# A perceiver block with a selective scan: the skip term moves from VectorE's first state to TensorE's open sums

## The chip, the core and the metric

The kernel runs on one core of one Trainium2 chip, in one launch. The metric is the device time of an execution in microseconds (us). In the profile PE is TensorE (PEld its weight loads), DVE is VectorE, ACT is ScalarE, POOL is GpSimd and SP is SyncE, which issues most DMAs.

## What is computed

The block has three parts, each with a layernorm before it and a residual after it: cross attention of 64 tokens per batch element on a context of 512 rows (16 batch elements, width 512), a selective scan, and a mixture of 16 experts with 4 chosen per token. The change touches the scan:

```
def step(h, inp):
    x_t, dt, B_t, C_t = inp
    A_disc = jnp.exp(dt[:, :, None] * A[None])
    h = A_disc * h + dt[:, :, None] * B_t[:, None, :] * x_t[:, :, None]
    y_t = jnp.einsum('bds,bs->bd', h, C_t) + D[None, :] * x_t
    return (h, y_t)
...
return y @ out_proj_w.T
```

There are 1024 inner channels and 16 states per channel. So y is a sum of 16 products (state times its C) and of the skip term D * x. All data is fp32.

## The kernel before, in words

**Groups.** The 1024 tokens are worked in four groups of 256. Tokens lie on the free axis and channels on the 128 partitions, so one state of one group is a tile of 128 x 2048 (8 blocks of channels by 256 tokens). The kernel is written out by hand for each engine; each engine has its own program, and semaphores join them.

**The scan of a group runs beside the attention of the next one.** For group g = 0, 1, 2 VectorE does the 16 states of group g while TensorE and ScalarE do the attention of group g + 1. The fourth group's scan runs beside the experts and does its sums on VectorE; it is not touched.

**One state** (scan_step, L1357 on) is on VectorE a product with B (L1365), a scan instruction that takes the decay and the product (L1368), and a product with C (L1372), which overwrites the decay's buffer. ScalarE makes the decay (scan_decay, 8 instructions at L1115). There are three decay buffers, so the decay of state n waits until TensorE has summed state n - 3. SyncE loads the B and C rows of each state (load_bc), two states ahead.

**The sum over states** is on TensorE (sum_state, L674): an identity matmul of the buffer into four PSUM banks, which stay open from the first state to the last. [...] The first state opens the banks (start = True). State 14 is not summed: VectorE adds it to state 15 (join_states, L1391), so a group has 15 sums. ScalarE copies the banks out at the end (copy_sum, L1090) and the output projection (L795) reads that.

**The skip term.** ScalarE writes D * x into th_tmp (y_start, L1082, semaphore ys_rdy). This buffer lies in the same memory as queries_ctx, which the next group's attention will fill. VectorE adds th_tmp to the product of the first state (add_skip, L1386, semaphore skip_added), after it has done states 0 and 1. Two engines wait for skip_added: TensorE before it sums the first state, and ScalarE before it overwrites the memory of th_tmp (L966).

**The order around a boundary**, for the attention of group g + 1:

- TensorE (attn_prep, L627 on): the query projection (16 matmuls, L637), a small key bias product (L643), from the third group on the routing logits of group g - 1 (ffn_logits: transposes L585, matmuls L605), then four steps c = 0 to 3 of the context queries (L665), with the sums of states 0, 1, 2 behind steps 1, 2, 3 (L687). Then two score products (L699) and the sum of state 3, and eight attention units with one sum each (L699, L687, the weighted context L720, the transposes of the probabilities L708).
- ScalarE (attn_prep, L939 on): copies of the queries (L948), the key bias (L981), the routing's copies (L908) and exponential (L923), then per step c the copies of the context queries (L966) and one decay: states 2, 3, 4, 5.
- VectorE: states 0 and 1, add_skip, from the second boundary on the routing of group g - 1 (route, from L1420 on, which waits for ScalarE's L923), states 2 and 3, then one state per unit beside the softmax pieces (L1300, L1304, L1354). In the second unit the slots of the routed tokens are worked out (L1461 to L1472), which wait for TensorE's positions (L621, L622, copied at L933).
- SyncE: the B and C rows wait for the state two before, the context loads for TensorE's scores. GpSimd clears DRAM rows during the first boundary (L1665).

Of the kernel before, what the change touches and what calls it, by code (L numbers as in the profile page):

```python
# [20 lines left out]
ALU = mybir.AluOpType  # L21
# [25 lines left out]
NBK = DI // P  # L47
NS = 16
# [11 lines left out]
GTS = [n * T for n in GBS]  # L60
# [44 lines left out]
JOINED = NS - 2  # L105
PE_SUMS = [j for j in range(NS) if j != JOINED]
NDEC = 3
# [45 lines left out]
def perceiver_block(nc, x, ctx_t, ctx_n, wq_t, wk_w, wv_t, xp_t, dt_t, bc_t, ow_t, gate_t,  # L153
                    eg_t, eu_t, ed_t, params, bc_dram, out):
    with ExitStack() as es:
# [3 lines left out]
        def sem(name):  # L159
            return es.enter_context(nc.semaphore(name))  # L160
# [14 lines left out]
        dA = [dA_[:, s * SW:(s + 1) * SW] for s in range(NDEC)]  # L175
# [8 lines left out]
        ident = par[:, C_ID:C_ID + P]  # L184
# [29 lines left out]
        with ExitStack() as early:  # L214
# [23 lines left out]
            th_tmp = [QT_[:, 3 * SW:3 * SW + NBK * GTS[g]] for g in range(NGR)]  # L238
# [45 lines left out]
        y_bank = bank[2:6]  # L284
# [52 lines left out]
        ys_rdy = sem("y_started")  # L337
# [1 line left out]
        scan_rd = sem("decay_read")  # L339
        step_done = sem("scan_step_done")  # L340
        state_summed = sem("state_summed")
        skip_added = sem("skip_term_added")
        joined = sem("state_joined")
        acc_rdy = sem("y_acc_copied")
        zero_rdy = sem("zero_rows_ready")
# [216 lines left out]
        def _(pe):  # L562
# [67 lines left out]
            def attn_prep(g):  # L630
                if g == 0:
                    pe.wait_ge(wq_in, 16)
                pe.wait_ge(a_free, ja.n)
                for m in range(DC):
                    b = job_a()
                    for c in range(DC):
                        mm = pe.matmul(b[:, 0:GTS[g]], wq[:, c, m * P:(m + 1) * P], xT[g][:, c, :],  # L637
                                       start=(c == 0), stop=(c == DC - 1))
                    mm.then_inc(a_full, 1)
                pe.wait_ge(a_free, ja.n)  # L640
                b = job_a()
                for m in range(DC):
                    mm = pe.matmul(b[0:H, 0:GTS[g]], par[:, C_BK + m * H:C_BK + (m + 1) * H], qT[g][:, m, :],  # L643
                                   start=(m == 0), stop=(m == DC - 1))
                mm.then_inc(a_full, 1)
                if g >= 2:
                    ffn_logits(g - 2)
                if g == 0:
                    pe.wait_ge(wk_in, 16)


                gt = GTS[g]
                pe.wait_ge(d_free, jd.n)
                for c in range(DC):
                    for mp in range(2):
                        if mp == 0:
                            pe.wait_ge(q_free, g * QPAIRS + c)
                            pair = X
                        else:
                            pair = job_a(), job_a()  # L660
                        for k in range(2):
                            m = 2 * mp + k
                            for hh in range(2):
                                r = slice(hh * DH, (hh + 1) * DH)
                                mm = pe.matmul(pair[hh][:, k * gt:(k + 1) * gt], wkt[r, m, c * P:(c + 1) * P],  # L665
                                               qT[g][r, m, :], start=True, stop=True)
                                if mp == 1 and k == 1:
                                    mm.then_inc(a_full, 1)
                        if mp == 0:
                            mm.then_inc(q_full, 1)  # L670
                    if g > 0 and c in (1, 2, 3):
                        sum_state(g - 1, c - 1)
                pe.wait_ge(q_free, (g + 1) * QPAIRS)
                pe.wait_ge(a_free, ja.n)  # L674

            def sum_state(g, j):

                if j == JOINED:
                    return
                if j == 0:  # L680
                    pe.wait_ge(skip_added, g + 1)
                elif j == JOINED + 1:
                    pe.wait_ge(joined, g + 1)
                else:
                    pe.wait_ge(step_done, g * NS + j + 1)
                for c in range(NBK * GTS[g] // 512):
                    mm = pe.matmul(y_bank[c][:, :], ident, dA[(g * NS + j) % NDEC][:, c * 512:(c + 1) * 512],  # L687
                                   start=(j == 0), stop=(j == NS - 1))
                mm.then_inc(state_summed, 1)

            def scores(g, k):
# [191 lines left out]
        def _(act):  # L883
# [60 lines left out]
            def attn_prep(g):  # L944
                for m in range(DC):
                    b = job_a()
                    o = qT[g][:, m, :].rearrange("p (b two i) -> p b i two", two=2, i=TI)
                    act.activation(o, b[:, 0:GTS[g]].rearrange("p (b i two) -> p b i two", two=2, i=TI), ACT.Identity,  # L948
                                   bias=par[:, C_BQ + m:C_BQ + m + 1], scale=DH ** -0.5).then_inc(a_free, 1)
                key_bias(g)  # L950
                if g >= 2:
                    ffn_copy(g - 2)
                    ffn_logits(g - 2)
                if g > 0:
                    act.wait_ge(skip_added, g)
                lead = list(range(2, LEAD + 2)) if g > 0 else []
                if len(lead) > DC:
                    scan_decay(g - 1, lead.pop(0))
                for c in range(DC):
                    q = QT[g][:, :, c, :].rearrange("p u (mp k hh i) -> p mp hh k u i", mp=2, k=2, hh=2)  # L960
                    for mp in range(2):
                        if mp == 0:
                            act.wait_ge(q_full, g * QPAIRS + c + 1)
                        for hh in range(2):
                            b = job_a() if mp else X[hh]
                            ins = act.activation(q[:, mp, hh], b[:, 0:2 * GTS[g]].rearrange("p (k u i) -> p k u i", k=2, u=NUS[g]),  # L966
                                                 ACT.Copy)
                            if mp:
                                ins.then_inc(a_free, 1)
                        if mp == 0:  # L970
                            ins.then_inc(q_free, 1)
                    if lead:
                        scan_decay(g - 1, lead.pop(0))
                assert not lead
# [268 lines left out]
        def _(dve):  # L1243
# [135 lines left out]
                    dve.tensor_tensor(acc_s[g], acc_s[g], h, ALU.add).then_inc(step_done, 1)  # L1379
                    dve.wait_ge(step_done, n + 1)  # L1380

            def add_skip(g):

                h = dA[g * NS % NDEC][:, 0:NBK * GTS[g]]
                dve.wait_ge(ys_rdy, g + 1)
                dve.tensor_tensor(h, h, th_tmp[g], ALU.add).then_inc(skip_added, 1)  # L1386

            def join_states(g):

                a, b = (dA[(g * NS + j) % NDEC][:, 0:NBK * GTS[g]] for j in (JOINED, JOINED + 1))  # L1390
# [181 lines left out]
            for g in range(NGR - 1):  # L1572
                for s in range(LEAD):
                    if s > 0:
                        scan_step(g, s)
                    if s == 1:
                        add_skip(g)
                    if s == 1 and g >= 1:
                        route(g - 1)
                for k in range(NUS[g + 1]):  # L1580
# [163 lines left out]
```

## Time and profile before

| | value |
|---|---|
| median of 3 runs | 1268.64 us (1268.61 to 1268.81) |
| the profiled execution's own time | 1268.13 us |
| its span | 1266.2 us (1.93 us lie around it) |
| instructions | 13226 |
| mean granted clock of TensorE | 0.946 of full speed |
| adds of the skip term (L1386) | 3, 6.9 us in all |
| sums on TensorE (L687) | 45, in 360 rows |

Times in the profile are microseconds from the span's start. A row of the timeline gives start, length, engine, line, operation and tiles, and in brackets how long the engine was idle before it and what it waited for. The chain of waits is followed back from the last instruction: at each step it names the piece of work that released the next one. The granted clock of 1.00 is 2.4 GHz for TensorE and 0.50 is 1.2 GHz; a value between is a mean over a stretch with both. A matmul's recorded end is modelled, so starts are the safer numbers on that engine.

### The profile page before, as it was taken

How to read it: one execution, taken by the hardware profiler on the slowest of the kernel's cores; microseconds unless marked ns; L12 is line 12 of the kernel's file. 1: busy time of each engine (PE TensorE's matmuls, PEld its weight loads, DVE VectorE, ACT ScalarE, POOL GpSimd, SP SyncE). 2: the span in 40 equal slices, each digit the busy share in tenths (PEclk: the TensorE clock that was granted, in tenths of full speed). 3: DMA queues.
4: the chain of work that ended last, by engine and by line, in shares of the span. 5: the costliest groups of instructions: out<-in, count | busy, mean ns of one | idle time of the engine just before them, and what ended most of it. 6: DMA issues, size and time to landing. Idle time of an engine off the chain costs nothing.

```text
span 1266.2 us, 13226 instructions
## 1 busy us (share of the span) xinstructions
PE 1109.1 (88%) x4228; PEld 711.6 (56%) x4228; DVE 895.3 (71%) x960; ACT 625.2 (49%) x1378; POOL 134.4 (11%) x113
## 2 busy tenths in 40 slices
PE   6997879998999999999799895459999999899992
PEld 4885646775755676656577582325544445454451
DVE  1312589999889999989989996569999956133312
ACT  4552676563666565586466454424555313222230
POOL 0001111000100340000070000210000002043002
PEclk9998889999999999999999998569999999999997
DMA  8368566768601454500344320279999957999994
GB/s 296 117 208 310 200 227 211 257 225 286 221 11 24 131 163 115 151 8 19 75 154 129 110 67 9 74 273 338 371 362 349 370 228 263 381 379 408 411 351 130
DMA packets 115187, 266.25 MB, mean 210 GB/s; under 512 B 11280, under 2 KB 44208, under 8 KB 115120
## 3 DMA queue, kind: packets, MB, share of 16 engines
q1 hardware_dynamic: 99248, 207.22, 47.9%
q0 software_dynamic: 15872, 58.20, 12.0%
q8 instruction: 34, 0.56, 0.2%
q14 instruction: 33, 0.27, 0.1%
HBM read 197.07 MB, written 68.32 MB: 210 GB/s over the span
## 4 chain that ended last, share of the span: by engine, by line
PE 55%; DVE 30%; ACT 6%; DMA 5%; issue 3%; POOL 1%; SPq 1%; POOLq 0%; DVEq 0%; ACTq 0%
PE bank L816 11%; DVE state L1368 10%; PE bank L777 9%; PE bank L720 6%; PE bank L699 6%; PE bank L837 6%; PE bank L687 6%; DVE state L1365 5%; PE bank L795 3%; DVE decay L1372 3%; PE bank L748 3%; DVE state L1375 2%; ACT decay L1115 2%; DMA queries_ctx<-in_xp_t 2%; DVE y_acc L1379 2%
## 5 line engine op out<-in xcount | busy, mean ns | idle before, releaser
L1368 DVE TENSOR_TENSOR_SCAN state<-decay,state 128x2048 f32<-128x2048 f32 x64 | 282.9, 4421 | 9.5 <-ACT decay L1115 8.6
L816 PE MATMUL bank<-expert_w,block_x_t 128*128 128x512 f32 x496 | 227.0, 601 | 3.8 <-ACT block_x_t L1171 3.8
L687 PE MATMUL bank<-decay,params 128*128 128x512 f32 x360 | 163.5, 600 | 4.5 <-DVE decay L1372 4.5
L816 PEld LDWEIGHTS bank<-expert_w,block_x_t 128*128 128x128 f32 x496 | 91.4, 194 | 95.7 <-issue 91.2
L1674 POOL DMA_INDIRECT dispatched<-ffn_x,slot x32 | 74.1, 2316 | 662.6 <-DVE slot L1472 654.0
L1115 ACT ACTIVATE decay<-delta_even,params 128x256 f32<-128x256 f32 x256 | 107.2, 498 | 49.4 <-PE bank L687 47.2
L720 PE MATMUL bank<-probs,ctx 128*128 128x256 f32 x512 | 121.3, 392 | 7.7 <-ACT probs L1012 7.7
L1527 DVE SCALAR_TENSOR_TENSOR hidden<-hidden,bank 128x256 f32<-128x256 f32 x62 | 26.1, 421 | 138.2 <-ACT hidden L1175 137.1
L699 PE MATMUL bank<-ctx,queries_ctx 128*128 128x256 f32 x512 | 118.3, 386 | 2.2 <-issue 1.2
L1115 ACT ACTIVATE decay<-delta_odd,params 128x256 f32<-128x256 f32 x256 | 106.2, 499 | 28.4 <-PE bank L687 25.1
L837 PE MATMUL bank<-expert_w,hidden_t 128*128 128x512 f32 x248 | 117.0, 594 | 2.9 <-ACT hidden_t L1185 2.9
L720 PEld LDWEIGHTS bank<-probs,ctx 128*128 128x128 f32 x512 | 100.4, 197 | 32.3 <-issue 10.0
L777 PE MATMUL bank<-normed_t,queries_ctx 128*128 128x256 f32 x512 | 112.1, 381 | 1.1 <-DMA queries_ctx<-in_xp_t 1.1
L687 PEld LDWEIGHTS bank<-decay,params 128*128 128x128 f32 x360 | 67.8, 192 | 77.5 <-issue 70.9
L1372 DVE TENSOR_TENSOR decay<-state,bc_bcast 128x2048 f32<-128x2048 f32 x48 | 109.5, 2281 | 0.7
L699 PEld LDWEIGHTS bank<-ctx,queries_ctx 128*128 128x128 f32 x512 | 97.3, 194 | 17.1 <-issue 3.1
L777 PEld LDWEIGHTS bank<-normed_t,queries_ctx 128*128 128x128 f32 x512 | 97.3, 191 | 16.4 <-DMA queries_ctx<-in_xp_t 2.5
L1175 ACT ACTIVATE hidden<-bank 128x256 f32<-128x256 f32 x62 | 23.7, 382 | 148.1 <-PE bank L816 148.1
L837 PEld LDWEIGHTS bank<-expert_w,hidden_t 128*128 128x128 f32 x248 | 46.8, 190 | 61.1 <-issue 57.4
L1181 ACT ACTIVATE block_y<-bank 128x512 f32<-128x512 f32 x62 | 37.1, 598 | 82.0 <-PE bank L837 82.0
L1365 DVE TENSOR_TENSOR state<-u_even,bc_bcast 128x2048 f32<-128x2048 f32 x32 | 73.3, 2291 | 4.0 <-DMA bc_bcast<-bc_scratch 3.1
L1365 DVE TENSOR_TENSOR state<-u_odd,bc_bcast 128x2048 f32<-128x2048 f32 x32 | 73.3, 2290 | 2.4 <-DMA bc_bcast<-bc_scratch 1.6
(192 smaller groups left out, 1327.9 us busy)
## 6 DMA issues: line engine op xcount, KB each, us to landing
dispatched<-ffn_x POOLq DMA_DIRECT2D x38, 1024.0 KB, 5.3
expert_w<-in_eg_t SPq DMA_DIRECT2D x62, 512.0 KB, 6.3
expert_w<-in_eu_t SPq DMA_DIRECT2D x62, 512.0 KB, 10.0
expert_w<-in_ed_t SPq DMA_DIRECT2D x62, 512.0 KB, 10.0
ctx<-in_ctx_t SPq DMA_DIRECT2D x32, 512.0 KB, 7.2
ctx<-in_ctx_n SPq DMA_DIRECT2D x32, 512.0 KB, 3.8
bc_bcast<-bc_scratch SPq DMA_DIRECT2D x64, 256.0 KB, 6.4
block_x<-dispatched SPq DMA_DIRECT2D x62, 256.0 KB, 9.8
```

What stands on the lines that cost most here:

```text
L687: mm = pe.matmul(y_bank[c][:, :], ident, dA[(g * NS + j) % NDEC][:, c * 512:(c + 1) * 512], start=(j == 0), stop=(j == NS - 1))
L699: mm = pe.matmul(o, QT[g][:, k, c, qb * P:(qb + 1) * P], ctxT[n % 2][:, c, :], start=(c == 0), stop=(c == DC - 1))
L720: mm = pe.matmul(b[:, cc * Q:(cc + 1) * Q], ctxN[n % 2][:, j, c * P:(c + 1) * P], probT[n % 2][:, j, :], start=(j == 0), stop=(j == KC - 1))
L748: mm = pe.matmul(b[hh * DH:(hh + 1) * DH, 0:GTS[g]], wv[:, c, h * DH:(h + 1) * DH], QT[g][:, :, c, h * TI:(h + 1) * TI], start=(c == 0), s ...
L777: mm = pe.matmul(b[:, kk * gt:(kk + 1) * gt], w[:, c, (k + kk) * P:(k + kk + 1) * P], xT[g][:, c, :], start=(c == 0), stop=(c == DC - 1))
L816: mm = pe.matmul(o, xbT[q % 2][:, c, :], w_gu[q % NW][:, :, c, :], start=(c == 0), stop=(c == DC - 1))
L837: mm = pe.matmul(bank[4 + q % 2][:, :], hidT[q % 2][:, c, :], w_dn[q % NW][:, c, :], start=(c == 0), stop=(c == IC - 1))
L1115: ins = act.activation(dA[n % NDEC][:, k * gt:(k + 1) * gt], dlt[g][:, k, :], ACT.Exp, scale=par[:, c:c + 1])
L1365: step(dve.tensor_tensor(h3, u[g], bs, ALU.mult))
L1368: dve.tensor_tensor_scan(h, dA[n % NDEC][:, 0:sw], h, 0.0, ALU.mult, ALU.add).then_inc(scan_rd, 1)
L1372: dve.tensor_tensor(hc, h3, cs, ALU.mult).then_inc(step_done, 1)
L1674: pool.indirect_dma_start(xd[WAVE_OF[c]], bass.IndirectOffsetOnAxis(slot[:, i:i + 1].bitcast(U32), 0), fx[:, t, :], None).then_inc(dispatc ...
```

## The change

The add of the skip term on VectorE is taken out, with its semaphore. TensorE puts th_tmp itself into the four banks with the identity, as an opening sum (start_sum), and the first state's sum is then added as the others are. The opening sum stands behind the key bias product and ahead of the routing logits. ScalarE no longer waits for skip_added before it fills queries_ctx; it waits for TensorE's context queries as before, and these stand behind the opening sum in TensorE's order. The joining of states 14 and 15 stays.

```
--- before.py
+++ after.py
@@ -339,7 +339,6 @@
-        skip_added = sem("skip_term_added")
@@ -643,6 +642,8 @@  (attn_prep of TensorE)
                 mm.then_inc(a_full, 1)
+                if g > 0:
+                    start_sum(g - 1)
                 if g >= 2:
                     ffn_logits(g - 2)
@@ -673,19 +674,23 @@
+            def start_sum(g):
+
+                pe.wait_ge(ys_rdy, g + 1)
+                for c in range(NBK * GTS[g] // 512):
+                    pe.matmul(y_bank[c][:, :], ident, th_tmp[g][:, c * 512:(c + 1) * 512], start=True, stop=False)
+
             def sum_state(g, j):
 
                 if j == JOINED:
                     return
-                if j == 0:
-                    pe.wait_ge(skip_added, g + 1)
-                elif j == JOINED + 1:
+                if j == JOINED + 1:
                     pe.wait_ge(joined, g + 1)
                 else:
                     pe.wait_ge(step_done, g * NS + j + 1)
                 for c in range(NBK * GTS[g] // 512):
                     mm = pe.matmul(y_bank[c][:, :], ident, dA[(g * NS + j) % NDEC][:, c * 512:(c + 1) * 512],
-                                   start=(j == 0), stop=(j == NS - 1))
+                                   start=False, stop=(j == NS - 1))
@@ -951,8 +956,6 @@  (attn_prep of ScalarE)
-                if g > 0:
-                    act.wait_ge(skip_added, g)
@@ -1378,12 +1381,6 @@
-            def add_skip(g):
-
-                h = dA[g * NS % NDEC][:, 0:NBK * GTS[g]]
-                dve.wait_ge(ys_rdy, g + 1)
-                dve.tensor_tensor(h, h, th_tmp[g], ALU.add).then_inc(skip_added, 1)
@@ -1573,8 +1570,6 @@  (main loop of VectorE)
                 for s in range(LEAD):
                     if s > 0:
                         scan_step(g, s)
-                    if s == 1:
-                        add_skip(g)
                     if s == 1 and g >= 1:
                         route(g - 1)
```

## Rows read from the trace of the kernel before

**Rows 1.** The page: busy time by engine, and the chain by engine.
```profile
PE 1109.1 (88%) x4228; PEld 711.6 (56%) x4228; DVE 895.3 (71%) x960; ACT 625.2 (49%) x1378; POOL 134.4 (11%) x113
...
PE 55%; DVE 30%; ACT 6%; DMA 5%; issue 3%; POOL 1%; SPq 1%; POOLq 0%; DVEq 0%; ACTq 0%
```

**Rows 2.** The instruction groups by line, of lines L687 and L1386.
```profile
L687 PE MATMUL bank<-decay,params 128*128 128x512 f32 x360 | 163.5, 600 | 4.5 <-DVE decay L1372 4.5
...
L1386 DVE TENSOR_TENSOR decay<-decay,queries_ctx 128x2048 f32<-128x2048 f32 x3 | 6.9, 2292 | 0.1
```

**Rows 3.** Chain of waits, stretch 150 to 300: shares, then start, length, piece.
```profile
by line: PE bank L687 23.3%; PE bank L699 18.3%; PE bank L720 17.4%; DVE state L1368 5.9%; DMA ctx<-in_ctx_t 5.9%; PE bank L748 5.2%; ACT decay L1115 4.4%; PE bank L665 4.0%; DVE decay L1372 3.1%; PE bank L708 1.9%; DVE u_even L1344 1.6%; D
...
176.52 2.30 DVE decay L1386
...
178.84 1.09 ACT queries_ctx L966 x2
...
179.98 2.21 PE bank L665 x16
...
203.88 3.45 PE bank L687 x8
```

**Rows 4.** Timeline, first boundary: start, length, engine, line, [idle before <- releaser].
```profile
160.43 3.28 ACT L1082 ACTIVATE queries_ctx<-queries_ctx,params 128x256 f32<-128x256 f32 x8
...
175.26 1.89 PE L643 MATMUL bank<-q_t,params 128*8 128x256 f32 x8 [0.82 <-ACT q_t L948]
...
177.09 2.01 PE L665 MATMUL bank<-q_t,attn_weights 64*128 64x256 f32 x16
...
180.77 3.30 ACT L1115 ACTIVATE decay<-delta_even,params 128x256 f32<-128x256 f32 x8
...
184.17 4.42 DVE L1368 TENSOR_TENSOR_SCAN state<-decay,state 128x2048 f32<-128x2048 f32 x1 [3.16 <-ACT decay L1115]
```

**Rows 5.** Timeline, second boundary, at the routing.
```profile
372.93 1.89 PE L643 MATMUL bank<-q_t,params 128*8 128x256 f32 x8 [0.80 <-ACT q_t L948]
...
378.14 2.29 DVE L1386 TENSOR_TENSOR decay<-decay,queries_ctx 128x2048 f32<-128x2048 f32 x1
...
379.13 0.20 ACT L923 ACTIVATE route_logits<-bank 128x32 f32<-128x32 f32 x1 [0.91 <-PE bank L605]
...
380.35 0.17 DVE L1420 TENSOR_SCALAR route_score<-route_logits 128x32 f32<-128x32 f32 x1
```

**Rows 6.** Timeline, third boundary, at the routing.
```profile
585.12 2.29 DVE L1386 TENSOR_TENSOR decay<-decay,queries_ctx 128x2048 f32<-128x2048 f32 x1
...
585.96 0.20 ACT L923 ACTIVATE route_logits<-bank 128x32 f32<-128x32 f32 x1 [0.71 <-PE bank L605]
...
587.33 0.17 DVE L1420 TENSOR_SCALAR route_score<-route_logits 128x32 f32<-128x32 f32 x1
```

**Rows 7.** Timeline, second group: the third state's sum, a transpose, the slots.
```profile
398.05 5.40 PE L687 MATMUL bank<-decay,params 128*128 128x512 f32 x8 [2.03 <-DVE decay L1372]
...
416.38 1.12 PE L708 MATMUL bank<-params,probs 128*128 128x128 f32 x4 [2.59 <-ACT probs L998]
...
429.84 0.19 DVE L1464 TENSOR_TENSOR route_position<-route_position,iota_f 128x32 f32<-128x32 f32 x1 [1.87 <-ACTq L935]
```

**Rows 8.** Timeline, third group: the same transpose.
```profile
623.07 0.66 PE L708 MATMUL bank<-params,probs 128*128 128x128 f32 x4 [3.99 <-ACT probs L998]
```

**Rows 9.** Chain of waits, whole run: the score matmuls behind those transposes.
```profile
210.57 3.46 PE bank L699 x16
...
417.50 4.57 PE bank L699 x16
...
623.72 5.14 PE bank L699 x16
```

**Rows 10.** Windows: PE, PEld, DVE, ACT, POOL busy, clock, DMA share, GB/s.
```profile
440.00:480.00 40.00, 39.87 (x163) 29.11 (x162) 39.31 (x29) 24.27 (x63) 18.48 (x6) 1.00 0.61 178
...
585.00:590.00 5.00, 5.00 (x31) 3.87 (x32) 4.66 (x18) 2.83 (x7) 0.00 (x0) 0.69 0.27 56
```

## The prediction, made before the changed kernel ran

> **What bounds the kernel now.** I read the page first, then the chain of waits, then the timeline of the three places where the change acts. The page gives PE 88% busy and DVE 71%, and the chain of the whole run is 55% PE and 30% DVE [rows 1]. So neither engine bounds alone, and an add taken from DVE and given to PE must be priced place by place. The add is made three times, 2.29 us each, and a sum on PE is eight rows of the trace [rows 2]; in an unbroken stream such a sum takes 3.45 us of PE's time [rows 3]. The change therefore trades 6.9 us of DVE for about 10.4 us of PE. Who is waited for at each of the three boundaries decides.
>
> At the **first boundary** the chain goes from the add (176.52) by ScalarE's copy (178.84) to PE at 179.98, and from there the stretch to 300 is mostly PE: its L687, L699 and L720 hold 59% of it [rows 3]. PE is what must not be delayed here. At the **second and third** the chain is DVE's: state 1, the add, the routing, states 2 and 3, without a gap that I can find up to the slots in the second unit. Here one looks at what DVE does next after the add: the routing's first instruction, L1420, which needs ScalarE's exponential L923, which needs PE's logits. The add ends at 380.43 and L1420 starts at 380.35 (the engine's pipeline overlaps them); L923 has ended at 379.33, only a microsecond before [rows 5]. At the third boundary it is 587.41, 587.33 and 586.16 [rows 6]. So the logits are nearly late already, and the change puts the opening sum ahead of them on PE.
>
> **First boundary, step by step.** The skip term is ready at 163.7 [rows 4], so the opening sum does not wait for it. The key bias product starts at 175.26 and the context queries follow it at 177.09 [rows 4]. The opening sum goes between them: 177.1 to 180.55. Step c = 0 then starts at 180.55 and has its first half (half of 2.01 us) done at 181.6. Today that half is done at 178.1, and ScalarE's copies begin at 178.84, held for 0.7 us by the add. So they would begin at about 181.7, and PE's step 1, which today starts at 179.98, 1.14 us behind them, would start at 182.85: **+2.9 us**. What is late next: the decay of state 2, today at 180.77, stands behind those copies on ScalarE and moves by 2.9 us too; DVE, which already waits 3.16 us for it at 184.17 [rows 4], then waits 2.9 + 2.3 us longer. Its own saving of 2.3 us is lost in that wait, and states 2 and on are 2.9 us late together with PE. The sums of states 0, 1 and 2 move by the same amount, none waits for another reason. Everything down to the group's end follows PE; I count 2.9 us in full. SyncE's loads of B and C and of the context wait for DVE's steps and PE's scores, so they move along; the key bias rows come from ahead of the opening sum and do not. GpSimd's clearing paces itself and costs nothing new.
>
> **Second boundary.** PE is at the key bias product at 372.93, with 1.89 us of it, and goes on to the routing's transposes [rows 5]. The skip term has long been there. With the opening sum ahead of them, transposes, ScalarE's copies, logits and L923 all come 3.45 us later: 379.33 becomes 382.8, and L1420 starts about 0.1 us behind, at 382.9 instead of 380.35: **+2.5 us** on DVE, which has been idle since 378.1. The 2.29 us saved turn into a wait of 4.8 us. Behind it the routing, state 2 and state 3 are 2.5 us late. PE's context queries are 3.45 us late, but PE waits 2.03 us for state 2 at 398.05 anyway [rows 7], so DVE's 2.5 us rule from there. At 416.38 PE waits 2.59 us for probabilities that hang on DVE's row sums and on the decay behind PE's fourth sum [rows 7], of which the second is a few tenths later; PE loses some 2.3 us there. In the units both engines are full: PE 39.87 of 40 us, DVE 39.31 [rows 10]. Nothing can catch up. I take **+2.4**.
>
> **Third boundary.** L923 ends at 586.16 and would end at 589.6; L1420 goes from 587.33 [rows 6] to 589.7: **+2.4**. The wait at 623.07, 3.99 us [rows 8], is for DVE alone, so it passes the delay on whole. ScalarE's wait for the add goes too, but it was held there for at most a tenth.
>
> **The sum** is 2.9 + 2.4 + 2.4 = 7.7 us. The taken-out add is worth nothing at all three places, since its engine waits for ScalarE or for the routing there. The first state's sum only changes its start flag, and joining, copying out and the output projection are as before: nothing. In the last group and the experts no instruction changes; they start later by the sum. Against the profiled execution, 1268.13 us, that is 1275.8 us; the median of the runs is 0.5 us above the profiled one, so **1276.3 us**.
>
> **Bounds of the unshown cost.** No row shows an opening sum at this place. From above: a sum at a lowered clock is also there, 5.40 us at 398.05 [rows 7], 1.95 us more than 3.45. At the routing each such case would cost 1.95 us. From below: zero, if PE did it in its own gaps. It can't, as PE works in order, but it is an end. I take 3.45 for all three: PE had been busy with dense matmuls just before. With zero at all three the change would gain: 0.7 us at the first boundary (the hold of the copies), 380.35 - 379.4 = 0.9 and 587.33 - 586.2 = 1.1 us, 2.7 us together.
>
> **A rule on the clock.** PE's granted clock is 0.69 between 585 and 590, just behind the broken run of small products and waits [rows 10], and the score matmuls behind the waits of 2.59 and 3.99 us take 4.57 and 5.14 us where an undisturbed set takes 3.46 [rows 9]. The opening sum adds 3.45 us of dense matmuls to that broken run and could keep the clock up; what that would give is rival B. The Trainium skill (TensorE: Matmul & The Clock Gate, the table "Why this matters for your kernels") says that idle gaps between bursts of matmuls let the clock fall back to half. By that rule this change would win some of these microseconds back; the trace agrees that they are lost today.
>
> **The rivals.**
>
> *A, forecast: PE's new sum is paid at all three places.* +7.7, 1276.3. Against it: it needs full occupation up to the slots. Its own range is 1274 to 1278.5.
>
> *B: the clock gives back.* If the sum keeps PE at full clock, L699 behind the two waits takes 3.46 instead of 4.57 and 5.14 [rows 9]: 1.1 and 1.7 us less. DVE waits 1.87 us for PE at the slots at 429.84 [rows 7], so it would pass on. +7.7 - 2.8 = +4.9, 1273.5. Against it: those waits are for DVE, and they get longer by the change, not shorter.
>
> *C: the sum itself runs at half clock* at the two routing places, +2 x 1.95 = +3.9: +11.6, 1280.2. For it: clocks do fall near there. Against: they fall after it.
>
> *D: hidden at the routing.* If DVE's delay were taken up by its wait of 1.87 us at the slots and its twin, only 0.5 us would be left at each of the two, and 2.9 at the first: +3.9 or less, down to no change if the first is also half hidden; 1269 to 1272. Against it: that wait is for positions that PE makes after the delayed probabilities.
>
> *E, the other side: faster.* The mechanism is the release of DVE. It is decided at L1420: if the logits are there at 378.1, DVE goes on at once. They come at 379.33 even without the opening sum, so the most is the 2.7 us above: 1265.9. It needs PE to have room for 3.45 us ahead of the logits, and its gap ahead of the key bias product is 0.80 us long [rows 5].
>
> *F: it does not do what it says*, a sum that is left out or done twice. The banks are opened once and the sixteen terms are still added; twelve new matmuls, 24 rows. I give it no chance of its own.
>
> **How the numbers follow.** A 0.70, B 0.11, C 0.07, D 0.09, E 0.03. What a measurement of this kernel can tell from no change is 0.2%, 2.5 us, so 1266.1 to 1271.2. All of A, B and C lie above: 0.88, with 0.02 of D 0.90 for slower. The rest of D is within: 0.07. E reaches the lower bound just so: 0.03 for faster. The range takes in A, B and most of C, and reaches down to the upper part of D: 1272 to 1280.
>
> **What would show it.** In the changed profile: L687 in 360 rows as before and a new line of 24, about 3.45 us for each eight; no L1386; at the first boundary PE's step 1 at about 182.9 and DVE's scan of state 2 at about 187.1 behind a wait of some 8 us; at the two others an idle DVE of 4.6 to 4.9 us ahead of L1420, and L1420 2.4 to 2.5 us later relative to the boundary. From the routing of the second boundary to that of the third it is 206.98 us today [rows 5, 6] and would be about 209.4. It is wrong if L1420 is not idle before it (then the logits don't wait for PE's order), if PE's units no longer fill, or if the experts' part changes in length by over a microsecond, since nothing there is touched.

## The result and the profile after

The changed kernel takes 1274.74 us, the kernel before 1269.05 us (medians of 20 runs each, taken side by side). The ratio is 1.0048, with a 95% interval of 1.0031 to 1.0064: 6.1 us slower, between 3.9 and 8.1 (the medians themselves are 5.7 us apart). Forecast were 7.7 us and 1276.3. Both kernels scatter more over 20 runs (1261 to 1272 and 1270 to 1279) than the first three runs of the kernel before showed. The profiled execution of the changed kernel took 1271.51 us, its span is 1269.6.

The page of the changed kernel, busy time and chain by engine. Its line numbers differ from those of the kernel before by three fewer to five more (the sum of a state, L687, is L692, the routing's first instruction, L1420, is L1417):

```profile
PE 1115.6 (88%) x4252; PEld 713.8 (56%) x4252; DVE 888.7 (70%) x957; ACT 624.2 (49%) x1378; POOL 134.2 (11%) x113
...
PE 62%; DVE 22%; ACT 6%; DMA 5%; issue 3%; POOL 1%; SPq 1%; POOLq 0%; DVEq 0%; ACTq 0%
```

The groups of instructions by line, TensorE's old and new sums:

```profile
L692 PE MATMUL bank<-decay,params 128*128 128x512 f32 x360 | 163.5, 600 | 3.6 <-DVE decay L1375 3.6
...
L681 PE MATMUL bank<-queries_ctx,params 128*128 128x512 f32 x24 | 11.1, 605 | 0.0
```

VectorE has three instructions and 6.6 us less, TensorE 24 rows more [rows 1, 2], two for each of the twelve matmuls. They take 11.1 us, of which TensorE's busy time shows 6.5, since other matmuls ran faster in this execution; and the chain has gone over to TensorE. The trade is the one forecast; the three places show what it costs.

The timeline of the first boundary (start, length, engine, line, idle time before):

```profile
174.19 1.89 PE L642 MATMUL bank<-q_t,params 128*8 128x256 f32 x8 [0.80 <-ACT q_t L953]
176.02 3.70 PE L681 MATMUL bank<-queries_ctx,params 128*128 128x512 f32 x8
179.65 2.00 PE L666 MATMUL bank<-q_t,attn_weights 64*128 64x256 f32 x16
180.83 2.06 ACT L969 ACTIVATE queries_ctx<-bank 128x512 f32<-128x512 f32 x4 [4.07 <-PE bank L666]
186.15 4.42 DVE L1371 TENSOR_TENSOR_SCAN state<-decay,state 128x2048 f32<-128x2048 f32 x1 [6.75 <-ACT decay L1118]
```

ScalarE's copies (L969) no longer wait for VectorE but for TensorE's context queries, which stand behind the sum (L681), and VectorE waits 6.75 us for the decay of state 2 instead of 3.16 [rows 4]. The waits are those that the forecast named, but TensorE's step 1 starts at 181.97 instead of 182.85, and VectorE's wait is 6.75 us instead of some 8.

The second boundary and the third (the sum's row is 3.70 us long with its modelled end, but the next row starts 3.54 us behind its start):

```profile
375.23 3.70 PE L681 MATMUL bank<-queries_ctx,params 128*128 128x512 f32 x8
...
378.77 1.04 PE L584 MATMUL bank<-params,ffn_x 128*128 128x128 f32 x8
...
382.65 0.20 ACT L928 ACTIVATE route_logits<-bank 128x32 f32<-128x32 f32 x1 [0.77 <-PE bank L604]
383.00 0.18 DVE L1417 TENSOR_SCALAR route_score<-route_logits 128x32 f32<-128x32 f32 x1 [4.42 <-ACTq L930]
...
400.71 3.70 PE L692 MATMUL bank<-decay,params 128*128 128x512 f32 x8 [1.05 <-DVE decay L1375]
...
592.69 0.18 DVE L1417 TENSOR_SCALAR route_score<-route_logits 128x32 f32<-128x32 f32 x1 [4.41 <-ACTq L930]
...
610.41 5.40 PE L692 MATMUL bank<-decay,params 128*128 128x512 f32 x8 [2.54 <-DVE decay L1375]
```

VectorE had no idle time ahead of the routing [rows 5, 6]; now it waits 4.42 and 4.41 us there for the logits. Against the start of the output projection before it (L795, now L800), the routing begins 31.53 and 31.55 us on, where it was 29.36 and 29.39: **2.2 us late at both**.

### The profile page after: what moved, and what is told of

Same layout as the page of the kernel before. It is cut to its first block, busy times and chain, and to the rows that moved or that the text cites. A ratio compares the mean times of both kernels' runs of the same rounds, so it can differ in the third digit from the quotient of the medians.

```text
span 1269.6 us, 13268 instructions
## 1 busy us (share of the span) xinstructions
PE 1115.6 (88%) x4252; PEld 713.8 (56%) x4252; DVE 888.7 (70%) x957; ACT 624.2 (49%) x1378; POOL 134.2 (11%) x113
## 4 chain that ended last, share of the span: by engine, by line
PE 62%; DVE 22%; ACT 6%; DMA 5%; issue 3%; POOL 1%; SPq 1%; POOLq 0%; DVEq 0%; ACTq 0%
PE bank L821 11%; PE bank L782 9%; DVE state L1371 7%; PE bank L692 7%; PE bank L725 7%; PE bank L704 7%; PE bank L842 6%; DVE state L1368 4%; PE bank L800 3%; PE bank L753 3%; PE bank L636 2%; ACT decay L1118 2%; DVE state L1378 2%; DMA queries_ctx<-in_xp_t 2%; DVE y_acc L1382 2%
## 5 line engine op out<-in xcount | busy, mean ns | idle before, releaser
L1371 DVE TENSOR_TENSOR_SCAN state<-decay,state 128x2048 f32<-128x2048 f32 x64 | 282.9, 4420 | 13.1 <-ACT decay L1118 12.2
L692 PE MATMUL bank<-decay,params 128*128 128x512 f32 x360 | 163.5, 600 | 3.6 <-DVE decay L1375 3.6
L725 PE MATMUL bank<-probs,ctx 128*128 128x256 f32 x512 | 117.9, 384 | 8.0 <-ACT probs L1015 8.0
L704 PE MATMUL bank<-ctx,queries_ctx 128*128 128x256 f32 x512 | 120.0, 390 | 1.3 <-issue 1.2
L725 PEld LDWEIGHTS bank<-probs,ctx 128*128 128x128 f32 x512 | 98.0, 192 | 31.7 <-issue 10.0
L692 PEld LDWEIGHTS bank<-decay,params 128*128 128x128 f32 x360 | 67.8, 192 | 76.5 <-issue 70.9
L704 PEld LDWEIGHTS bank<-ctx,queries_ctx 128*128 128x128 f32 x512 | 98.8, 197 | 16.6 <-issue 3.1
```

The source lines that it names most:

```text
L704: mm = pe.matmul(o, QT[g][:, k, c, qb * P:(qb + 1) * P], ctxT[n % 2][:, c, :], start=(c == 0), stop=(c == DC - 1))
L725: mm = pe.matmul(b[:, cc * Q:(cc + 1) * Q], ctxN[n % 2][:, j, c * P:(c + 1) * P], probT[n % 2][:, j, :], start=(j == 0), stop=(j == KC - 1))
L1371: dve.tensor_tensor_scan(h, dA[n % NDEC][:, 0:sw], h, 0.0, ALU.mult, ALU.add).then_inc(scan_rd, 1)
```

## The experiments

Twelve further runs came in three batches, a, b and c, each batch with the kernel before on the same chip; a1 is the change again and c4 is b4 again. Each of the twelve was timed 12 times, a2 only 6 times. Since single executions scatter by several microseconds, each row below also has starts from its one profile. *Scores 1* is the start of the first score product behind the start of the first scan (the memset L1348); *routing* and *scores* 2 and 3 count from the start of the output projection (L795) that opens the boundary. *Length* is the sum of the three groups, from that memset to the third output projection. "Against before" is the ratio of the timed runs times 1269 us, with its interval.

| kernel | scores 1 | routing 2 | scores 2 | routing 3 | scores 3 | length | against before, us |
|---|---|---|---|---|---|---|---|
| before | 39.67 | 29.36 | 52.30 | 29.39 | 50.64 | 608.5 | |
| the change, first profile | 41.06 | 31.53 | 52.78 | 31.55 | 54.51 | 612.1 | +6.1 (3.9 to 8.1) |
| a1, the change again | 41.29 | 31.54 | 52.79 | 31.55 | 52.82 | 613.6 | +5.3 (2.7 to 7.9) |
| a2, sum twice | 44.62 | 35.18 | 56.44 | 34.99 | 57.96 | 622.3 | +13.1 (9.5 to 16.8) |
| a3, logits first | 41.07 | 28.90 | 53.88 | 28.37 | 52.25 | 609.7 | +0.8 (-2.2 to 3.6) |
| a4, no skip term | 37.54 | 30.04 | 53.00 | 28.38 | 49.64 | 602.5 | -4.2 (-6.7 to -1.5) |
| b1, first group alone | 41.88 | 29.35 | 52.29 | 29.38 | 50.61 | 610.3 | +2.8 (0.4 to 5.2) |
| b2, the two others alone | 39.67 | 31.74 | 52.98 | 31.55 | 54.50 | 609.6 | +6.6 (3.9 to 9.3) |
| b3, b2 with logits first | 39.66 | 28.36 | 50.54 | 28.38 | 52.26 | 607.0 | +0.5 (-2.2 to 3.0) |
| b4, ScalarE into the banks | 39.07 | 28.28 | 49.52 | 28.28 | 49.52 | 605.5 | -2.0 (-4.4 to 0.3) |
| c1, early first sum, logits first | 37.09 | 28.61 | 52.23 | 28.37 | 52.25 | 605.5 | -3.7 (-5.8 to -1.6) |
| c2, early first sum alone | 37.12 | 29.35 | 52.30 | 29.39 | 50.64 | 605.6 | -2.0 (-4.8 to 0.6) |
| c3, sum ahead of the key bias | 40.03 | 30.92 | 52.18 | 31.54 | 52.80 | 612.0 | +3.7 (1.1 to 6.1) |
| c4, b4 again | 37.39 | 28.62 | 49.89 | 28.27 | 51.24 | 602.3 | -2.7 (-5.2 to -0.1) |

The two *scores* columns of the later boundaries also carry the clock under the sum of state 2, which stands just ahead: it takes 3.70 us in some profiles and 5.40 in others, 1.7 us with no edit in it. At the second boundary it took 5.40 in the kernel before, a4, b1 and c2, at the third in the change's first profile, a2, b2 and c4. A later start is mostly free of that: the transposes in the second unit (L708, now L713), where TensorE has waited for the probabilities. Behind the output projection they start at 65.39 and 65.13 in the kernel before [rows 7, 8], at 67.27 and 67.61 in the change, at 67.29 and 67.31 in a1. That is 1.9 and 2.5, and 1.9 and 2.2 us late: the delay of the routing arrives there. The third group's row in the changed kernel:

```profile
628.75 1.11 PE L713 MATMUL bank<-params,probs 128*128 128x128 f32 x4 [2.59 <-ACT probs L1001]
```

**a1: the change once more.**

> The change itself once more, beside the others of this batch. Theory (TensorE's new sum is paid at all three boundaries: about 2.9 us at the first, where TensorE is the bound, and about 2.4 us at each of the two others, where VectorE waits at L1417 for logits that stand behind the sum): +6 to +7.7 us against the kernel before. Rival (the sum is paid at the first boundary alone, +2.9, and the rest is chance between runs): +3.

+5.3 us, between the two, and the interval holds 6 to 7.7 as well as 3. The routing starts where it did in the first profile, to 0.01 us.

**a2: the opening sum twice.** In start_sum:

```
-                for c in range(NBK * GTS[g] // 512):
-                    pe.matmul(y_bank[c][:, :], ident, th_tmp[g][:, c * 512:(c + 1) * 512], start=True, stop=False)
+                for again in (True, False):
+                    for c in range(NBK * GTS[g] // 512):
+                        pe.matmul(y_bank[c][:, :], ident, th_tmp[g][:, c * 512:(c + 1) * 512], start=True, stop=again)
```

> The opening sum is issued twice at its place; the result is the same. Theory: each boundary loses 3.45 us more, +10.3 us over the change, +16 to +18 over the kernel before; VectorE idle ahead of L1417 about 7.9 us instead of 4.4. Rival (first boundary alone): +3.5 over the change. Rival (hidden in TensorE's waits further on): under +2.

7.8 us over a1, against 10.3 expected: less than the theory, more than the rivals. Its timeline at the second and third boundary:

```profile
391.39 0.18 DVE L1418 TENSOR_SCALAR route_score<-route_logits 128x32 f32<-128x32 f32 x1 [8.06 <-ACTq L931]
...
603.80 0.18 DVE L1418 TENSOR_SCALAR route_score<-route_logits 128x32 f32<-128x32 f32 x1 [7.84 <-ACTq L931]
```

The wait grows by 3.6 and 3.4 us, the sum's own time, and the scores of all three boundaries move by 3.3 to 5.1 us against a1 (1.7 of the 5.1 are the clock under the sum of state 2). In the lengths, of one profile each, the second sum costs 8.7 us. Where the rest of the 10.3 is taken up is not shown.

**a3: the logits first.** In attn_prep of TensorE:

```
-                if g > 0:
-                    start_sum(g - 1)
                 if g >= 2:
                     ffn_logits(g - 2)
+                if g > 0:
+                    start_sum(g - 1)
```

> The opening sum stands behind the routing logits. Theory (the place ahead of the logits is what costs at the second and third boundary): VectorE goes on at L1417 with an idle time of 0.9 to 1.1 us instead of 4.4, and both boundaries are 0.9 to 1.1 us shorter than in the kernel before; with +2.9 at the first that is about +1 against before and -5 to -6 against the change. Rival (TensorE's 10.4 us of work count wherever they stand, since its units are full): within 1 us of the change.

+0.8, the theory's number; 4.5 us of a1's cost are gone with nothing but the order. But the parts are not the theory's, so that the number agrees is partly chance: the first boundary costs 1.4 us instead of 2.9, and the two others do not give the 0.9 to 1.1 us each. The wait ahead of the routing is short, though longer than expected, and the routing starts earlier than in the kernel before (28.90 and 28.37):

```profile
380.76 0.18 DVE L1417 TENSOR_SCALAR route_score<-route_logits 128x32 f32<-128x32 f32 x1 [1.78 <-ACTq L930]
...
587.24 0.18 DVE L1417 TENSOR_SCALAR route_score<-route_logits 128x32 f32<-128x32 f32 x1 [1.22 <-ACTq L930]
```

But TensorE's scores then start 1.6 us later than before (53.88 and 52.25), and what the routing gained does not arrive. Its rows at the two boundaries show why:

```profile
380.21 6.49 PE L681 MATMUL bank<-queries_ctx,params 128*128 128x512 f32 x8
...
586.71 5.38 PE L681 MATMUL bank<-queries_ctx,params 128*128 128x512 f32 x8
```

Behind the small products the granted clock is 0.56 and 0.68 while the sum runs, and the sum takes 6.49 and 5.38 us instead of 3.5. TensorE comes too late for the sum of state 2: it used to wait 2.03 and 2.52 us for VectorE there and now does not wait. At the second boundary VectorE too waits 1.50 us, for ScalarE's decay of state 2, which stands behind the late context queries. That part the theory had left out.

**a4: no skip term.** The computation leaves D * x out; add_skip and start_sum are gone, and the first state opens the banks (start=(j == 0)). ScalarE still writes the term, which nothing reads.

> The skip term is left out altogether: no add on VectorE, no opening sum; the first state opens the banks. Theory: what the skip term cost before is only 0.7 us (first boundary, copies held) and 0.9 to 1.1 us (each routing), 2.7 us in all, though 6.9 us of VectorE's work are gone: -2.7 against before. Rival (VectorE is the bound at the second and third boundary and 2.3 us a piece come back): -5 to -7.

-4.2, between the two. The third boundary gives 1.0 us at the routing, as computed; the second gives none in this profile (30.04), where the output projection ahead of it takes 15.67 us instead of 13.99. The first gives 2.1 us at the scores, three times the 0.7 of the forecast, with a query projection that was quicker than in the kernel before (see the section on why the prediction was right).

**b1 and b2: the boundaries apart.** A constant names the groups that have the opening sum; the others keep add_skip, its semaphore and the two waits as in the kernel before. In attn_prep of TensorE (OPENED is (0,) in b1 and (1, 2) in b2):

```
-                if g > 0:
+                if g - 1 in OPENED:
                     start_sum(g - 1)
```

> TensorE's opening sum for the first group alone; the second and third keep VectorE's add in the first state. Theory (each boundary pays for itself): only the first boundary changes, +2 to +3 us against before. Rival (the first boundary costs nothing, its delay is taken up before the group's end): within 1 us of before.

> The opening sum for the second and third group alone, ahead of the routing logits; the first keeps VectorE's add. Theory: +2.2 us at each of two boundaries, +4 to +5 against before; L1417's twin idles about 4.4 us at both. Rival (first boundary alone pays): within 1 us of before.

b1 measured +2.8 and has the second and third boundary of the kernel before to 0.03 us in every column. So the first boundary pays alone. b2 measured +6.6, more than the theory's 4 to 5, with an interval that holds it, and 31.74 and 31.55 at the routing. The two together are 9.4, over the change's 6.1 and 5.3; the intervals are wide enough for that, and the lengths of b1 and b2 are 1.8 and 1.1 us over the kernel before's, where the change's are 3.6 and 5.1. b2's timeline shows what the kernel before does at the first boundary when the query projection is quick:

```profile
181.09 2.06 ACT L982 ACTIVATE queries_ctx<-bank 128x512 f32<-128x512 f32 x4 [2.05 <-DVE decay L1402]
182.22 2.21 PE L675 MATMUL bank<-q_t,attn_weights 64*128 64x256 f32 x16 [1.91 <-ACT queries_ctx L982]
```

TensorE waits 1.91 us for copies that wait for VectorE's add. In the profile of the forecast it was 0.88, because the second half of the query projection took 6.76 us there and 5.74 here.

**b3: b2 with the logits first** (both edits above).

> The opening sum for the second and third group alone and behind the routing logits; the first keeps VectorE's add. Theory: the first boundary is as before, the two others are 0.5 to 1.0 us shorter at the routing, and TensorE's sum lies in its wait for state 2: -1 to -2 against before. Rival (TensorE's units are full, so its added 6.9 us count in part): 0 to +3.

+0.5: the rival's band, though its interval reaches to the theory's. The routing gains 1.0 us twice. At the second boundary the scores come 1.8 us earlier than before, at the third 1.6 us later. Two sums make the difference. The sum of state 2 starts no earlier than before at the second (47.00 and 47.06 us behind the output projection) but takes 3.70 us instead of 5.40; and the opening sum runs at a granted clock of 1.00 at the second and 0.68 at the third, where it makes TensorE late for state 2:

```profile
378.73 3.68 PE L690 MATMUL bank<-queries_ctx,params 128*128 128x512 f32 x8
...
584.41 5.38 PE L690 MATMUL bank<-queries_ctx,params 128*128 128x512 f32 x8
```

**b4 and c4: ScalarE writes the skip term into the banks.** From the kernel of a4; not shown are three smaller edits: the zeros (seed_zero) are filled once, ScalarE signals each bank that it has copied out instead of all four together, and the first state's sum waits for ys_rdy.

```
+            def open_banks(g):
+
+                for c in range(NBK * GTS[g] // 512):
+                    if g:
+                        pe.wait_ge(acc_rdy, 4 * (g - 1) + c + 1)
+                    mm = pe.matmul(y_bank[c][:, :], seed_w[:, :], seed_v, start=True, stop=False)
+                mm.then_inc(opened, 1)
...
+                if g in SUMMED:
+                    act.wait_ge(opened, g + 1)
...
-                    ins = act.activation(o[:, at], th_tmp[g][:, at], ACT.Copy, scale=par[:, C_D + k:C_D + k + 1])
+                    col = k * GTS[g]
+                    o = y_bank[col // 512][:, col % 512:col % 512 + GTS[g]] if g in SUMMED else acc_s[g][:, at]
+                    ins = act.activation(o, th_tmp[g][:, at], ACT.Copy, scale=par[:, C_D + k:C_D + k + 1])
```

> Neither VectorE nor TensorE adds the skip term: ScalarE writes D * x straight into the four PSUM banks instead of into its buffer, and the states are summed on top. TensorE opens the banks first with four matmuls of zeros in bf16 (128 x 512), for the first group in its wait for the transposes, for the other two in its wait for ScalarE's copies. Theory: as without the skip term, which measured -4.2 us against before, less some 0.3 us at two places: -3 to -4.2. Rival (the write to PSUM or the new wait of ScalarE for the opening delays the first decays): 0 or slower.

> ScalarE's write into the opened banks once more, to narrow its interval: -2 to -4 against before by the theory and by its first measurement; within 1 us of before if that one was chance.

-2.0 and -2.7, less than the theory had. Both intervals lie below zero but for a few tenths of the first, and both hold -3 to -4.2 as well. The profile of b4 at the first group:

```profile
146.24 1.03 PE L683 MATMUL bank<-seed_zero 128*128 128x512 bf16 x4
...
160.23 3.25 ACT L1096 ACTIVATE bank<-queries_ctx,params 128x256 f32<-128x256 f32 x8
```

Opening four banks takes 1.03 us in bf16, and writing D * x to PSUM takes ScalarE the 3.25 us that it took to SBUF (3.28 in [rows 4]). So the add and the sum are gone for a microsecond of TensorE per group. Whether that recovers all of a4's 4.2 us the intervals cannot tell.

**c1 and c2: the first group's sum where TensorE waits.** In the query projection; c1 has in addition the logits first for the other two groups, c2 leaves them VectorE's add.

```
                 for m in range(DC):
+                    if g == 1 and m == 2:
+                        start_sum(0)
                     b = job_a()
```

> All three groups have TensorE's opening sum, but the first one's stands in the middle of the query projection, where TensorE waits 7 to 8 us for ScalarE, and the two others' behind the routing logits. Theory (the place decides, the work does not): the first boundary reaches its scores about 2 us earlier than before (as without the skip term), the two others come out as in the run with the logits first, so -1 to -3 against before. Rival (a sum on TensorE costs its time wherever it is): +5.

> Only the first group has the opening sum, in that early place; the two others keep VectorE's add. Theory: the first boundary 2 us shorter, the rest as before: -2. Rival: as the first group's sum in the place of the change, +2.8.

-3.7 and -2.0, with the scores of the first boundary 2.6 us earlier than before in both. c1 is clear of no change and a little beyond its theory, which its interval holds; c2's interval reaches to +0.6. The timeline of c1:

```profile
163.20 5.23 PE L683 MATMUL bank<-queries_ctx,params 128*128 128x512 f32 x8 [3.07 <-ACT queries_ctx L1087]
...
168.27 3.62 PE L638 MATMUL bank<-normed_t,attn_weights 128*128 128x256 f32 x16
```

The sum lies in a wait that was 6.92 us long in the kernel before, and the second half of the query projection behind it takes 3.62 us where it took 6.76 and 5.11 in the profiles of the kernel before and of the change. The granted clock there is 1.00 in c1 and in c2, 0.55 in the kernel before and 0.72 in the change. The sum is not quite free there: the projection's second half starts 11.7 us behind the scan's start instead of 10.6, and only its higher clock makes up for that. c1 does the same work as the change and beats both it and the kernel before: the interval ends at -1.6.

**c3: the sum one product earlier.** start_sum stands ahead of the wait for the last copied queries instead of behind the key bias product.

> The change with the opening sum one product earlier, ahead of TensorE's wait for the last copied queries. Theory (the logits wait for TensorE in order, and only idle time ahead of them can hide a part): the wait of 0.80 us is filled, so the routing starts about 0.8 us earlier than in the change (30.8 us behind the output projection instead of 31.55), and the whole is about 2 us faster than the change, +3 to +4 against before. Rival (all 3.45 us are hidden or none): +5 to +6 or 0.

+3.7, as expected, with an interval that also holds the change's 5.3; and the profile agrees only at the second boundary, 30.92 instead of 31.54. At the third the routing is where it was, 31.54. Its timeline there:

```profile
582.07 3.60 PE L681 MATMUL bank<-queries_ctx,params 128*128 128x512 f32 x8
585.59 1.89 PE L644 MATMUL bank<-q_t,params 128*8 128x256 f32 x8
587.42 1.44 PE L584 MATMUL bank<-params,ffn_x 128*128 128x128 f32 x8
589.68 2.53 PE L604 MATMUL bank<-gate_weights,probs 128*128 128x16 f32 x16 [0.82 <-ACTq L920]
```

The wait of 0.80 us is filled, but the two products behind take 1.44 and 2.53 us instead of 1.04 and 1.93. The first difference is no matter of the clock, which is 1.00 under these transposes in all profiles: with the key bias product right ahead of them they wait for ScalarE again (see below), here and at the second boundary. The second is the clock, which fell earlier. Windows of c3 and of the change over the same stretch (PE, PEld, DVE, ACT, POOL busy, clock, DMA share, GB/s):

```profile
590.00:595.00 5.00, 5.00 (x29) 4.45 (x30) 2.13 (x15) 1.87 (x4) 0.00 (x0) 0.58 0.28 43
```

```profile
590.00:595.00 5.00, 4.30 (x36) 3.75 (x38) 2.07 (x14) 3.25 (x7) 0.00 (x0) 1.00 0.22 45
```

So its timed gain on the change can't be laid on the filled wait alone.

## Why the prediction was right, step by step

**Direction and mechanism** held. The add's 2.29 us of VectorE came back nowhere: VectorE waits instead for the decay of state 2 (6.75 us) and for the logits (4.42 and 4.41 us; 4.6 to 4.9 were given). a3 shows by the order alone that the place ahead of the logits costs most of it, b1 that the first boundary pays for itself, a2 that each further 3.45 us arrive at the routing in full, and the transposes of the second unit that the delay of the routing goes on from there (1.9 and 2.5 us; the forecast took some 2.3 and 2.4).

**First boundary, forecast +2.9.** The scores come 1.4, 1.6 and 2.2 us late in the three profiles (the change, a1, b1). The scores of the kernel before start at 39.67 whether the second half of its query projection is slow (6.76 us, rows of the forecast) or quick (5.74 and 5.87 us in b2 and b3), since VectorE's add sets them; with a quick projection TensorE's wait is 1.91 us. With the opening sum in place the scores follow the projection instead, which took 5.11, 5.34 and 5.93 us in those three profiles. Carried on to 6.76 us, an estimate from the change's row, they would be 3.0 us late. So the step "ScalarE's copies begin at 178.84, held for 0.7 us by the add" was right for its own profile, in which the granted clock was 0.55 under the projection, and too small for the profiles of the change. The add's price there depends on the same thing. b4 and c4 are one kernel, without the add, and their scores come 0.6 and 2.3 us earlier than the kernel before's; their projections:

```profile
167.46 6.76 PE L639 MATMUL bank<-normed_t,attn_weights 128*128 128x256 f32 x16 [6.89 <-ACT q_t L961]
```

```profile
168.04 5.10 PE L639 MATMUL bank<-normed_t,attn_weights 128*128 128x256 f32 x16 [8.56 <-ACT q_t L961]
```

**Second and third, forecast +2.5 and +2.4 at the routing:** 2.17 and 2.16. The sum took its 3.5 us; but the transposes behind it ran in 1.04 instead of 1.45 us. The granted clock is 1.00 under them in both kernels, so this is not rival B. In the kernel before the second four of them waited for ScalarE's copy of the key bias product (L981), and behind the sum that copy is long done. The forecast had no such wait. The weight load of these four, third boundary of the kernel before:

```profile
582.51 0.42 PEld L585 LDWEIGHTS bank<-params,ffn_x 128*128 128x128 f32 x4 [0.36 <-ACT probs L981]
```

Rival B's mechanism, a clock that gives back, did occur in another place: the sum of state 2 at the second boundary takes 3.70 us in the change, a1, a2 and b2, and 5.40 in the kernel before [rows 7], b1 and c2. That is why the scores there are only 0.5 us late. It is no gain, since TensorE then waits longer for the probabilities, 3.99 us instead of 2.59. At the third boundary it went the other way, 5.40 us instead of 3.70, and not in a1. Where B had it, behind the waits for the probabilities, it did not come in the second group, where L704 behind L713 takes 5.43 us, more than the 4.57 [rows 9]; in the third it takes 4.54 instead of 5.14. The row of L713 in the timeline of the changed kernel, and of L704 in its chain:

```profile
418.74 1.11 PE L713 MATMUL bank<-params,probs 128*128 128x128 f32 x4 [3.99 <-ACT probs L1001]
```

```profile
419.85 5.43 PE bank L704 x16
```

**The sum.** 1.4 to 2.2 at the first and 2.2 at each of the two others make 5.8 to 6.6; measured were 6.1 and 5.3. Forecast was 7.7: too large by the hold (about 1 us) and by the transposes' wait (0.3 us each). The hold was read in a profile with a slow projection, 6.76 us, which only two of the twelve profiles without a sum ahead of it have. Rival C (the sum itself at half clock; its figure, 1280.2, lies just outside the stated range, of which the forecast said that it takes in most of C) did not occur in the change, 11.1 us for three sums, but it did behind the logits (a3, b3). Rival D is out by a2 and b2. Rival E's most, 2.7 us, was too small at its first term, for the same reason as the hold: leaving the term out gives 4.2 in all, and c1 reached 3.7 with the sum in place, by a way that I had not looked at, the wait inside the query projection. The intervals of both hold 2.7, so this rests on the starts.

**Signs that were set badly.** The experts' part was to change by no more than 1 us. It is 500.6 us long in the kernel before, 499.8 in the change and 498.2 in a1, and no edit touches it. From the second routing to the third 209.4 us were forecast: 209.7 in the change, 207.3 in a1. Neither sign can tell this edit from the scatter between profiles.

**What stays open.** b1 and b2 add up to 3 us more than the change; with intervals of 2.5 us on each that may be chance, and no run here settles it. Why the clock falls under one sum and not under its twin (3.70 and 5.40 us for state 2, 3.68 and 5.38 in b3) is open too.

## What to carry to other kernels

When work is moved to an engine that works in order, look first at what stands behind the new place and who waits for it: the same three sums cost 6 us with two of them ahead of the logits and 1 us with these behind, and with the first one in a wait too the kernel was 3.7 us faster than before. And ask what wait the removed operation was hiding or causing: read it in more than one profile, because a wait next to matmuls changes with the clock. If an engine already makes a term that is to be summed in PSUM, having it write there can save the add and the sum (b4 and c4, 2.0 and 2.7 us faster, the second just clear of no change); here TensorE opened the banks first.

## What the runs showed that was not expected

**The clock moves the parts by 1 to 2 us from run to run.** The same 16 rows of L725 near the end of a group, in the chain of the changed kernel (start, length, piece):

```profile
497.43 5.42 PE bank L725 x16
...
707.79 3.73 PE bank L725 x16
```

The kernel before has 5.42 us in both groups. In the second half of the first query projection the spread is 5.10 to 6.76 us over the profiles without a sum ahead of it. Groups two and three of the change and of a1 have the same edits and the same routing, and yet are 209.7 and 208.7 us long in the one and 207.3 and 211.7 in the other. The part behind the third output projection, which no edit touches, was 497.1 us (a2) to 506.4 us (b3) long; what moves it was not looked into. That is why a profile's span alone (here 1269.6 against 1266.2, 3.4 us) is a poor measure of an edit of this size, and the start of one instruction behind a near anchor, which mostly repeats to 0.02 us at the routing, is a good one, as long as nothing in between changes its clock (a4).

**Filling a wait with matmuls went both ways.** In c3, with 0.80 us filled, the granted clock was 0.58 in a stretch at the third boundary where the change, with the same sum 3 us later, had 1.00. In c1 and c2, with the sum in the long wait of the first query projection, the clock was 1.00 under its second half, which took 3.62 us in both; no profile without that sum has it under 5.10. Two profiles against twelve are an indication; whether the filled wait is the cause is not shown.
